# Batch 0's tiles first in the first FFN, and its way into the second attention moved into the tile slots

## The reference, cut to what matters

```python
x = x + attn_a(layernorm(x), Mq, Mk, Mv)            # 8 heads of 64
x = x + ffn(layernorm(x), w_gate, b_gate, W1, b1, W2, b2)
x = x + attn_b(layernorm(x), wq, w_down, wk_up, wv_up, wo)   # 16 heads of 8, rope, page mask
x = x + ffn(layernorm(x), w_gate, b_gate, W1, b1, W2, b2)

def ffn(x):                                          # 8 experts, the best one for each row
    probs = softmax(x @ w_gate + b_gate)
    h = relu(x @ W1[e] + b1[e]); y = h @ W2[e] + b2[e]     # 128 -> 512 -> 128
    return y[argmax(probs)] * max(probs)

def attn_b(x):                                       # each batch for itself
    q, lat = x @ wq, x @ w_down
    k, v = rope(lat @ wk_up), lat @ wv_up;  q = rope(q)
    return softmax(mask(q k^T / sqrt(8))) v @ wo
```

## Time and profile before

| | |
|---|---|
| median of three runs | 492.01 us |
| the profiled execution's own time | 490.57 us |
| its span | 488.7 us |
| first FFN, first tile's transpose to the last tile's output | 150.37 to 202.62 us |
| last output to the start of round 0 | 202.62 to 253.38 us |
| second FFN, the same stretch | 421.03 to 475.3 us |

### The profile page before, as it was taken

The page is one execution under the profiler, slowest core; times in us unless marked ns, Lnnn a source line. Parts: engine busy times, 40 slices in busy tenths (PEclk is TensorE's granted clock), DMA queues, the critical chain, the costliest instruction groups (busy, mean ns, idle before and its releaser), DMA issues.

```text
span 488.7 us, 15624 instructions
## 1 busy us (share of the span) xinstructions
PE 411.0 (84%) x5250; PEld 320.9 (66%) x5251; DVE 309.4 (63%) x1125; ACT 231.5 (47%) x565; POOL 214.2 (44%) x312
## 2 busy tenths in 40 slices
PE   8898899998657899977679989989888888698980
PEld 7777588885547899854446555655555567598880
DVE  4776588888564555369557568568877655454543
ACT  2687556766304555211226756756655420255540
POOL 5443345555641444325643635643822434133440
PEclk9999999999769999988858999999999876799995
DMA  8999900000001121120000000000000000112116
GB/s 237 297 217 347 275 15 9 7 11 12 24 16 45 56 65 54 40 85 1 2 1 2 1 1 3 1 0 0 1 2 7 30 23 22 35 50 64 55 48 182
DMA packets 44339, 28.60 MB, mean 59 GB/s; under 512 B 7200, under 2 KB 40480, under 8 KB 44288
## 3 DMA queue, kind: packets, MB, share of 16 engines
q1 hardware_dynamic: 38096, 20.83, 15.4%
q0 software_dynamic: 2496, 5.13, 2.9%
q10 hardware_dynamic: 3696, 1.97, 1.4%
HBM read 12.76 MB, written 15.16 MB: 57 GB/s over the span
## 4 chain that ended last, share of the span: by engine, by line
PE 58%; DVE 17%; issue 8%; DMA 7%; ACT 5%; DVEq 2%; POOL 2%; SPq 0%; POOLq 0%; ACTq 0%
PE S L1435 7%; PE bank L1445 6%; PE S L1343 6%; PE bank L1302 6%; PE bank L1319 3%; PE bank L1475 3%; PE bank L1558 3%; DVE nm L756 3%; DMA slots<-yo,token 2%; PE bank L1329 2%; PE bank L1248 2%; PE bank L1569 2%; PE bank L1254 2%; PE S L1275 2%; DMA xg<-rows 2%
## 5 line engine op out<-in xcount | busy, mean ns | idle before, releaser
L915 ACT ACTIVATE E<-S,nmax 128x256 f32<-128x256 f32 x128 | 59.0, 477 | 39.2 <-DVE nmax L541 39.2
L1148 POOL DMA_INDIRECT slots<-yo,token x46 | 44.1, 958 | 75.5 <-DVE yo L697 74.1
L1011 ACT ACTIVATE E<-S 128x1536 f32<-128x1536 f32 x32 | 46.4, 1450 | 24.4 <-PE S L1534 24.3
L1107 POOL TENSOR_TENSOR vs<-Va,rden 128x512 f32<-128x512 f32 x32 | 33.3, 1040 | 50.5 <-DVE rden L576 48.6
L1435 PE MATMUL S<-xgT,W1s 128*128 128x128 f32 x368 | 52.9, 289 | 1.4 <-DVE xgT L683 1.3
L972 ACT ACTIVATE hT<-S,b 128x128 f32<-128x128 f32 x92 | 28.7, 363 | 44.2 <-PE S L1435 44.2
L1445 PE MATMUL bank<-W,hT 128*128 x368 | 49.2, 277 | 0.2
L1435 PEld LDWEIGHTS S<-xgT,W1s 128*128 128x128 f32 x368 | 46.2, 197 | 4.5 <-issue 2.2
L756 DVE TENSOR_REDUCE nm<-bank 128x2 f32<-128x512 f32 x64 | 41.0, 683 | 9.1 <-PE bank L1501 9.1
L1445 PEld LDWEIGHTS bank<-W,hT 128*128 128x128 f32 x368 | 45.2, 194 | 0.5 <-issue 0.5
L541 DVE TENSOR_REDUCE nmax<-S 128x4 f32<-128x1024 f32 x32 | 39.0, 1218 | 7.2 <-PE S L1343 6.8
(11 more groups left out here) (181 smaller groups left out, 954.9 us busy)
## 6 DMA issues: line engine op xcount, KB each, us to landing
rows<-zeros SPq DMA_DIRECT2D x1, 8768.0 KB, 31.5
xg<-rows SPq DMA_DIRECT2D x46, 64.5 KB
W<-in_L_ffn_W SPq DMA_DIRECT2D x1, 2048.0 KB, 10.2
x<-in_L_attn_a_x SPq DMA_DIRECT2D x4, 256.0 KB, 5.4
yg<-slots SPq DMA_DIRECT2D x8, 128.0 KB, 3.5
yg<-slots ACTq DMA_DIRECT2D x8, 128.0 KB, 3.9
slots<-yo,token POOLq DMA_INDIRECT x46
yg<-in_select SPq DMA_DIRECT2D x1, 512.0 KB, 7.8
```

Of the source, the lines that this page charges most:

```text
L915: last = act.activation(E[:, hp, h, c, :], S[hp % 2][:, h, c * T:(c + 1) * T], ACT.Exp, bias=nmax[:, hp, k:k + 1], accum_out=den[:, hp, k: ...
L1011: act.activation(Eb[:, q % 2, :, :], S4[:, 0:3, :], ACT.Exp, scale=SCALE_B).then_inc(bs["exp"], 1)
L1107: pool.tensor_tensor(vs[:, q, :, :, :], v, r, ALU.mult).then_inc(a_vs, 1)
L1148: pool.indirect_dma_start(out=y_dram, out_offset=bass.IndirectOffsetOnAxis(token[:, turn_at, :], 0), in_=yo[:, turn_at % 2, :], in_offset=None
```

## The change

- The table has 16 segments rather than 8: first, expert by expert, the tiles that hold rows of batch 0, then, expert by expert, the others. For this `sofar` keeps the count after every batch. In the second FFN the first segments are those of batches 0 to 3, and nothing else is changed in its slots.
- Batch 0 is complete after 9 slots at the most. Its return is loaded in slot 12, and its add, statistics, norm, transpose, projections, rotation, split and repeat stand in slots 13 to 23.
- The first FFN's slots are written out, with no loop, on all engines. All its outputs go to bank 2, so each output matmul waits for the `yo` before it.
- After the tiles the scores of batch 0 come at once. The returns of batches 1 to 7 stand between its maxima. SyncE loads them all.
- Round -1 is gone; its work stands in the code ahead of round 0.
- The norm ahead of the second attention is applied by ScalarE (two activations with a scale and a shift, `norm_scale`). GpSimd works out the shift too: four instructions a batch rather than two.
- `b_parts` works on q and k one after the other: 10 instructions rather than 9. Batches 2 and 3 no longer need `b_stage`.

```diff
+EARLY = (1, 4)
+EARLY_SLOTS = tuple((k * 2 * P + NE * (P - 1)) // P for k in EARLY)     # 9, 15
@@ b_rounds
-            for b in (-1, 0):
-                round_(b, b % 2)
+            round_(0, 0)
@@ slot_steps(eng, step, last, after=None)
+            if after:
+                for s in range(-1, last + 1):
+                    held = step(s, s % TURN, held)
+                    after(s)
+                return
@@ sync
-                ffn_return(sp, n, 0)
+                ffn_return(sp, n, SLOTS, range(1, B) if n == 0 else range(0, B, 2))
@@ vector: ffn_table (13 linked instructions and row, where there were 9 and row)
+                link(dve.tensor_tensor(above[:, :, :, :], pb[3][:, 3 * NE:5 * NE]..., const("steps")..., ALU.is_gt))
+                link(dve.tensor_reduce(upto[:, :]..., above[:, :, :, :], AX.X, ALU.add))
...
@@ vector, after ffn_weights(0)
+            def returned(c):
+                ffn_add(0, c)
+                dve.wait_ge(ffn[0]["x"], 2 * c + 2)
+                waits(dve, norm[2]["rstd"], c - 1)
+                norm_stats(2, c, c % 2)
-            for c in range(B + 1):
-                if c < B:
-                    ffn_add(0, c)
-                    dve.wait_ge(ffn[0]["x"], 2 * c + 2)
-                    norm_stats(2, c, c % 2)
-                if c > 0:
-                    norm_apply(2, c - 1, (c - 1) % 2)
-                if c == 2: b_turn_q(0)
...
+            def early(s):
+                k = s - EARLY_SLOTS[0] - 4
+                if k == 0: returned(0)
+                if k == 4: b_turn_q(0)
+                if k == 5:
+                    dve.wait_ge(bs["turnq"], 1)
+                    b_parts(dve, chain0, 0, 0, 0)
+                if k == 6: b_turn_k(0)
...
+                if k == 10:
+                    b_parts(dve, chain0, 0, 1, 2)
+                    dve.sem_inc(bs["split"], 1)
+                    b_repeat(0, 0)
+            ffn_tiles(0, early)
+            returned(1)
+            b_max(0, 0)
+            returned(2)
+            b_max(0, 1)
+            b_turn_q(1)
+            b_max(0, 2)
+            returned(3)
+            b_turn_k(1)
+            b_max(0, 3)
+            returned(4)
+            b_turn_q(2)
+            returned(5)
+            b_turn_k(2)
+            returned(6)
+            returned(7)
+            b_repeat(1, 1)
             b_rounds(dve, b_round)
@@ scalar
+            def norm_scale(c, p):
+                act.wait_ge(s["rstd"], c + 1)
+                for u in range(2):
+                    last = act.activation(normed(2, c, p)[:, u, :], x[:, 2 * c + u, :], ACT.Identity,
+                                          bias=shift[:, p, u:u + 1], scale=rstd[:, p, u:u + 1])
+            def early(s):
+                k = s - EARLY_SLOTS[0] - 3
+                if k == 0: ffn_return(act, 0, EARLY_SLOTS[0], range(1))
+                if k == 2: norm_scale(0, 0)
+                if k == 3: norm_out(2, 0, 0, pb[3])
+                if k == 4: b_latent(0)
+                if k == 6: b_v(0, 0)
@@ gpsimd
+            def early(s):
+                if s == EARLY_SLOTS[0] + 4: inverse_deviation(2, 0, 0)
+            ffn_tiles(0, early)
+            b_place_v(0, 0)
+            inverse_deviation(2, 1, 1)
+            inverse_deviation(2, 2, 0)
+            b_split(1, 1, lambda: inverse_deviation(2, 3, 1))
+            b_maxima(0)
+            for c in range(4, B):
+                inverse_deviation(2, c, c % 2)
@@ tensor
-                        waits(pe, f["yo"], s - 2)
+                        waits(pe, f["yo"], s - (1 if n == 0 else 2))
-            ffn_tiles(0)
-            keep_busy(18, 3)
+            def early(s):
+                k = s - EARLY_SLOTS[0] - 6
+                if k == 0: norm_transpose(2, 0, 0, pb[3])
+                if k == 1: b_q(0, 0)
+                if k == 3: b_kv(0)
+            ffn_tiles(0, early)
+            keep_busy(6, 2)
+            b_tq(0, 0, 0)
+            b_tk(0, 0, 0)
+            b_scores(0, 0, 0)
+            b_tq(0, 0, 1)
+            b_scores(0, 0, 1)
+            b_tk(0, 0, 1)
+            returned(1)                 # norm_transpose(2, c), keep_busy(2)
+            b_scores(0, 0, 2)
+            b_q(1, 1)
+            returned(2)
+            b_kv(1)
+            b_scores(0, 0, 3)
+            b_q(2, 0)
+            b_kv(2)
+            b_max_transpose(0)
+            for c in range(3, B):
+                returned(c)
             b_rounds(pe, b_round)
```

More of the change, by code:

```diff
@@ L395, in load @@
                     sp.dma_start(xg[:, par, :], rows[bass.ds(at, P), :]).then_inc(f[f"in{par}"], 16)
+                if n == 0:
+                    for s in range(SLOTS):
+                        load(s, s % 2)
+                    return
                 load(0, 0)
@@ new lines, in ffn_table @@
+                link(dve.tensor_reduce(upto[:, :].rearrange("p (l e) -> p l e", e=NE), above[:, :, :, :], AX.X, ALU.add))
+                chain.inc(dve.tensor_copy(many[:, 0:NE], upto[:, 0:NE]))
+                link(dve.tensor_tensor(many[:, NE:SEGS], upto[:, NE:SEGS], upto[:, 0:NE], ALU.subtract))
+                chain.inc(dve.scalar_tensor_tensor(out=skip[:, :], in0=upto[:, :], scalar=-float(P), in1=const("gap"),
+                                                   op0=ALU.mult, op1=ALU.add))
@@ L1136, in _, with ffn_tiles @@
             scatter(0, 7, 1)
[L1137 to L1140 removed]
+            def ffn_tiles(n, after=None):
                 f = ffn[n]
@@ L1169, in b_split @@
                 waits(pool, bs["tk"], b * 2 - 2)
-                for k in range(3):
-                    b_parts(pool, chain, p, k)
-                assert chain.k == 9
+                for i in range(2):
+                    pool.wait_ge(bs[("turnq", "turnk")[i]], b + 1)
+                    for k in range(3):
+                        b_parts(pool, chain, p, i, k)
+                    if between and i == 0: between()
+                assert chain.k == 10
                 pool.sem_inc(bs["split"], 1)
@@ L1563, in b_values, with b_max_transpose @@
                 last.then_inc(bs["pv"], 1)
+            def b_max_transpose(b):
+                pe.wait_ge(bs["ms"], b + 1)
+                for u in range(2):
+                    last = pe.transpose(pb[2][:, 0:P].bitcast(BF16)[:, u * P:(u + 1) * P], ms[:, u, :], identb[:, :])
+                last.then_inc(bs["mt"], 1)
             def b_natural(b, p, u):
@@ L1641, in b_round @@
                 if n:
-                    pe.wait_ge(bs["ms"], b + 2)
-                    for u in range(2):
-                        last = pe.transpose(pb[2][:, 0:P].bitcast(BF16)[:, u * P:(u + 1) * P], ms[:, u, :], identb[:, :])
-                    last.then_inc(bs["mt"], 1)
+                    b_max_transpose(b + 1)
                 if isinstance(b, int) and b == 7:
@@ L1720, in _constants @@
     cols["region"] = np.where(i[:, None] == 0, REGION * np.arange(NE), 0)
+    gap = np.full(SEGS, REGION)
+    gap[NE - 1::NE] -= NE * REGION
+    cols["gap"] = np.tile(gap, (P, 1))
     cols["steps"] = np.tile((REGION * np.arange(NE)[:, None] + P * np.arange(NT)).reshape(1, -1), (P, 1))
```

253 lines of the change are left out of this document (139 added, 114 removed).

## The result

The changed kernel takes 491.0 us (median of 20 runs, 486.29 to 499.88), the kernel before 494.11 us (20 runs, 489.76 to 502.46). The ratio is 0.9929 (95% interval 0.99 to 0.9959): 3.5 us faster (2.0 to 4.9). The forecast was 7.2 us. A second comparison with 12 runs of the changed kernel gave 0.9965 (0.9922 to 1.0008), an interval that still holds no change at all.

The account below looks back on a forecast made before the run. TensorE was taken to pace the first FFN's slots, and a chain of hand-overs the 50.76 us before round 0. Terms +0.5 + 0.2 - 1.6 + 6.9 + 0.2 - 12.2 - 1.5 + 0.3 = -7.2 gave 484.8 us from 492.0, range 478.5 to 491.5.

Parts of the forecast that it names:

- Part 3: Slots 13 to 23, first FFN: batch 0's added work makes engines wait for each other, +6.9 us (bounds 0 to +17).
- the walk: Engine-by-engine count of hand-overs, giving 29.6 us for slots 13 to 23 and 38.6 from last output to round 0.
- Part 4: From last output to round 0: 38.6 us instead of 50.76, -12.2, with a new 3.4 us VectorE wait.
- Part 2: First FFN's slots 3 to 12 without a loop: loop turn and step savings, -1.6 us; early single-bank wait +0.2.
- Part 1: Longer table ahead of the tiles: +0.5 us at the start, +0.3 second FFN, +0.2 for counts in first attention.
- Round 0: First round behind the open stretch: TensorE starts warmer, so it gets faster by 1.5 us (0 to -3).
- The first (slots absorb the work): Slots 13 to 23 pay only +2 us for batch 0's work: sum -12, 480 us; chance 0.22.
- The second (clock): TensorE falls to 1.2 GHz in the new stretch's gaps, into round 0: +0.7, about 492.7 us; chance 0.09.
- The third (GpSimd's powers held up): GpSimd's powers meet VectorE's adds and parts in slots and stretch, +5 us: sum -2.2, 489.8; chance 0.09.
- The fourth (slots as one chain): Nothing overlaps in slots 13 to 23, which cost +17 us: sum +2.9, 495 us; chance 0.08.
- the fifth: Tile order does nothing for batch 0, as if its return landed late; chance 0.02 together with others.

Follow-up runs that it names:

- the written-out slots: The kernel before with only the first FFN's slots written out on all engines, two output banks kept: 491.07 us, ratio 0.9973.
- the combined kernel: The changed kernel with batch 0's norm before tile 13's scatter, two output banks, third maxima earlier, idle matmuls only behind batches 3 to 7: 480.7 us, ratio 0.9724.

## Why the prediction was wrong

The mechanisms came as forecast, and the gain was half of it, because TensorE's clock was put at its full rate in three places where it fell: behind its wait in slots 13 to 23, at the start of the slots, and ahead of batch 1's latent. The largest miss is Part 3: +6.9 us in the sum, +9.2 measured.

- **Part 3: the walk was right, its clock was missing.** The waits came in the forecast order at the forecast places, for `xgT` (1.02 us for 1.7) and at the transpose (2.47 for 2.9), and batch 0's return was in time (0.20 us). But the walk let TensorE go on at full clock after standing still, while Part 4 of the same prediction counted a lower clock after gaps. The one profile in which TensorE did keep its clock took 29.93 us for the walk's 29.6; the two of the changed kernel took 31.91 and 31.98. That it came so close is in part luck: the two waits were 1.1 us shorter than walked, and the single output bank, put at nothing, made the steps longer. With the wait taken out by one number, the slots took 26.90 us. So +6.9 was really +4.2 for the work and +5.0 for one hand-over queued behind a scatter and what followed from it.
- **Part 2 had no term for a start at 1.2 GHz.** Seven profiles have the changed kernel's slots 0 to 12 as they are. Three of them had no group at 1.2 GHz in the first steps and took 27.62, 27.63 and 28.03 us, a mean of 27.76 against 29.45 before: -1.7 for the forecast -1.4. One had two such groups (28.96), and three had three or more (30.50, 30.54 and 30.62). The mean of all is 29.13: -0.3. Neither profile of before had one, nor that of the written-out slots. That the later first tile behind the longer table causes it is possible and wasn't isolated.
- **The single output bank was put at nothing.** That was argued from `yo` being done in time, which it is, and still a step takes 2.07 us instead of 1.90. In slots 13 to 23 as they stand two banks gave 0.6 us; in slots 0 to 12 late loads can take the gain away (29.25 us in the combined kernel).
- **Part 1 was right** (+0.6 at the start for +0.5, +0.4 in the second FFN for +0.3), but for the +0.2 in the first attention, which no stage can show.
- **Part 4: the mechanism was right, the size 1.1 us off.** VectorE's new wait was 5.73 us for 3.4, because batch 1's latent came 1.8 us later than in the walk. The low clock was counted (+2.5), but at the second projection and the last transposes; the trace has it also at batch 1's transpose, idle matmuls and projection. The sum gave 38.6; measured was 39.6 to 39.8.
- **Round 0 was right** (-1.8 for -1.5), and in this kernel the idle matmuls give it: without them it runs at 0.82 and takes 17.80 us.
- **Of the rivals** none is the whole answer. The first (slots absorb the work) is ruled out as the change stands. The second (clock) was looked for in the stretch and round 0, and sat in the slots and at batch 1's latent. The third (GpSimd's powers held up) didn't happen: batch 0's norm took 1.4 us from 189.92 to 191.33, as costed, and all eight powers took 0.69 to 0.72 us. What showed instead: VectorE's two adds at 234.69, beside GpSimd's split, took 1.41 us instead of 0.61. The Trainium skill, page "SBUF — State Buffer", section "Who interferes with whom", says that such a pair of instructions contends; the trace agrees there. The fourth (slots as one chain) didn't happen: they took 31.9 us, not 37. Nor did the fifth: the return was in time.
- **The range.** The measured 491.0 us lies within 478.5 to 491.5, near its end. The kernel before took 494.11 us in the comparison, where the forecast started from 492.0; 3.5 us off 492.0 is 488.5. The gain itself was half of the forecast one: three terms leaned the same way, each had been taken at its likeliest value, and unknown ones at nothing.

## What to carry to other kernels

When a chain is laid into a full stretch of work, follow each hand-over to the engine's queue it stands in; one that stands behind an instruction waiting for something else costs its wait and can cost TensorE's clock behind it as well, here 3.0 us with the clock kept and 5.0 with it lost, for one position in GpSimd's order. A shared buffer whose wait is always met in time in the trace isn't proven free: compare the step with and without it. Idle matmuls are paid for on the path as well: by the stages they gave round 0 1.5 us here and added 2.0 to the stretch ahead of it, so count both.

## What the runs showed of the hardware

- TensorE stood still for 2.47 us in the middle of full-clock work in five profiles. In four it ran the next two groups at 1.2 GHz (2.05 and 1.79 us in the first) and the granted clock of slots 13 to 23 was 0.95; in the fifth it stayed at 2.4 GHz (1.13 and 1.06 us, 1.00). Waits of 0.95 to 1.44 us for `xgT`, a step or two earlier, left it at 2.4 in all nine profiles that have them.
- The start of the slots differed between executions of the same instructions, by 2.8 us from the mean of those at full clock to the slowest three. The idle time just ahead of the first tile doesn't order them: 1.2 GHz from the first group after 1.26 us (the second profile of the changed kernel), 2.4 GHz throughout after 1.71 us (the kernel with batch 0 behind the slots), and 2.4 GHz for one group, then 1.2, after 2.26 us (the first profile of the changed kernel).
- A wait that had been met 0.6 us earlier went with a step 0.17 us longer.
